# Sampling by matrix product in batches of three: twelve transposes, then three gathers, on six banks, with the exponent's table loaded at the start

## The reference

```
pos_y = base_y + inner_y + off_y            # clipped to 0 .. 17, the same for x
value = (hh*hw*v1 + hh*lw*v2 + lh*hw*v3 + lh*lw*v4) * mask
out   = einsum('nhwc,cf->nhwf', value, w)   # 9 taps x 64 channels -> 64
...
attn  = softmax(q @ k.T / sqrt(32));  o = attn @ v
...
c = h * c + sigmoid(i) * tanh(g);     h = sigmoid(o) * tanh(c)     # 256 steps
```

## Time and profile before

| | us |
|---|---|
| median of three runs | 424.03 (423.84 to 425.36) |
| the profiled execution | 425.57 |
| its span, first to last instruction | 423.8 |
| TensorE busy in the span | 399.5 (94%) |
| ScalarE busy | 262.9 (62%) |
| VectorE busy | 240.2 (57%) |
| GpSimd busy | 59.3 (14%) |
| mean granted TensorE clock | 0.994 of full |

### The profile page before, as it was taken

How to read it: one execution, slowest core, us unless ns; L and a number is a source line. 1 busy time by engine, 2 the same in 40 slices (tenths; PEclk the granted TensorE clock), 3 DMA queues, 4 the chain that set the end, 5 groups by cost and what they waited for, 6 DMA issues and landing times.

```text
span 423.8 us, 14792 instructions
## 1 busy us (share of the span) xinstructions
PE 399.5 (94%) x5669; PEld 215.5 (51%) x5669; DVE 240.2 (57%) x1161; ACT 262.9 (62%) x1127; POOL 59.3 (14%) x131
## 2 busy tenths in 40 slices
PE   8999998888999899999999999999899999999996
PEld 2555553545455455545555554555455545554332
DVE  2477745154565566656565656665566656565443
ACT  1676643563786587568748865876587568744443
POOL 6000004001111111012111102111111012110000
PEclk9999998999999999999999999999999999999999
DMA  7000000000000000000000000000000000000000
GB/s 243 0 2 2 2 2 0 0 2 2 3 3 2 4 6 2 4 2 5 5 2 5 4 2 4 5 3 3 2 6 3 2 2 7 3 3 5 2 2 5
DMA packets 2244, 3.78 MB, mean 9 GB/s; under 512 B 1277, under 2 KB 1726, under 8 KB 2174
## 3 DMA queue, kind: packets, MB, share of 16 engines
q1 hardware_dynamic: 1872, 2.32, 1.8%
q10 hardware_dynamic: 302, 0.52, 0.4%
HBM read 2.57 MB, written 0.26 MB: 7 GB/s over the span
## 4 chain that ended last, share of the span: by engine, by line
PE 69%; DVE 12%; ACT 12%; issue 5%; DMA 1%; POOL 1%; DVEq 0%
PE bank L349 20%; PE bank L620 15%; PE bank L478 7%; DVE bank L1036 5%; PE bank L416 5%; PE bank L404 5%; PE bank L489 4%; DVE H L1046 4%; ACT bank L760 4%; PE bank L506 3%; ACT bank L753 3%; PE bank L377 2%; ACT E L734 2%; ACT QB L726 2%; PE bank L518 1%
## 5 line engine op out<-in xcount | busy, mean ns | idle before, releaser
L349 PE MATMUL bank<-FB 128*128 128x512 bf16 (+3 forms) x677 | 184.4, 369 | 1.2 <-DVE FB L786 1.2
L620 PEld LDWEIGHTS bank<-H,VW 128*32 128x32 f32 x3072 | 53.0, 109 | 92.9 <-DVE H L1046 88.1
L620 PE MATMUL bank<-H,VW 128*32 128x4 f32 x3072 | 75.6, 179 | 12.6 <-DVE H L1046 5.6
L1036 DVE TENSOR_TENSOR_SCAN bank<-bank,SU 64x12 f32<-64x12 f32 x256 | 48.7, 190 | 64.9 <-ACT bank L753 62.2
L753 ACT ACTIVATE bank<-bank 64x8 f32<-64x8 f32 x256 | 37.9, 148 | 73.1 <-PE bank L620 72.1
L1046 DVE SCALAR_TENSOR_TENSOR H<-TO,bank 64x4 f32<-64x4 f32 x256 | 40.9, 160 | 49.2 <-ACT bank L760 47.4
L349 PEld LDWEIGHTS bank<-FB 128*128 128x128 bf16 x677 | 50.9, 99 | 31.4 <-issue 5.7
L760 ACT ACTIVATE bank<-bank 64x4 f32<-64x4 f32 x256 | 38.8, 152 | 17.6 <-DVE bank L1036 2.9
L757 ACT ACTIVATE TO<-bank 64x4 f32<-64x4 f32 x256 | 44.1, 172 | 6.3
L1030 DVE SCALAR_TENSOR_TENSOR SU<-H,bank 64x4 f32<-64x4 f32 x256 | 41.4, 162 | 9.0
L333 POOL TENSOR_SCALAR E<-E,rinv 128x256 f32<-128x256 f32 x56 | 27.0, 481 | 139.5 <-DVE rinv L909 139.5
(11 more groups left out here) (117 smaller groups left out, 341.1 us busy)
## 6 DMA issues: line engine op xcount, KB each, us to landing
AW<-in_attn_w SPq DMA_DIRECT2D x1, 768.5 KB, 8.1
DW<-in_dcn_w SPq DMA_DIRECT2D x1, 576.0 KB, 6.7
X<-in_x_fm SPq DMA_DIRECT2D x1, 256.0 KB, 3.3
X<-in_x_fm ACTq DMA_DIRECT2D x1, 256.0 KB, 5.2
out_dram<-OUT SPq DMA_DIRECT2D x8, 32.0 KB, 1.4
CW<-in_conv_w SPq DMA_DIRECT2D x1, 243.5 KB, 4.2
VEC<-in_vecs SPq DMA_DIRECT2D x1, 160.0 KB, 8.0
K<-in_consts ACTq DMA_DIRECT2D x1, 154.0 KB, 3.6
```

Of the source, the lines that this page charges most:

```text
L349: nc.tensor.matmul(idle[:, 0:n], FB[:, 0:P], FB[:, 0:n], start=True, stop=True)
L620: mm = nc.tensor.matmul(gate_out(m, gate, r, slice(B * s, B * (s + 1))), VW[:, gate, r], H[:, (STEPS * m + s - 1) % RING, :], start=False, ...
L1036: nc.vector.tensor_tensor_scan(CS.rearrange("p b q -> p (b q)"), GT.rearrange("p b q -> p (b q)"), SU[:].rearrange("p b q -> p (b q)"), 0. ...
```

## The change

Groups go through TensorE in threes. The loop issues the turns of three groups (twelve transposes), then the three gathers of the batch before. The first batch's turns are followed directly by the second's, and the last two batches' gathers stand together at the end. A, AT and the banks of the transposes become rings of six, and all waits that guard a slot are moved from 3 or 4 groups back to 6. The bank ring is now banks 1, 2, 0, 3, 6, 7; since Z went through banks 0, 3, 6 and 7, the wait for its 16 copies moves from gather(0) to turn(2) up to turn(5).

The second edit is a table load for Exp at the top of ScalarE's program, behind its three DMA issues; the load of the first tile at L763 is left out (`m > 0`).

```
+BATCH = 3
+SLOTS = 2 * BATCH
...
-        A = sb("A", [P, 4, HALVES, N])
-        AT = sb("AT", [P, 4, 2, HALVES, P])
+        A = sb("A", [P, SLOTS, HALVES, N])
+        AT = sb("AT", [P, SLOTS, 2, HALVES, P])
...
-        b_at = banks[1:4]
+        b_at = banks[1:3] + banks[0:1] + banks[3:4] + banks[6:8]
...
-                if g >= 3:
-                    pe.wait_ge(at_sb, g - 2)
+                if 2 <= g < SLOTS:
+                    pe.wait_ge(z_sb, 4 * B)
+                elif g >= SLOTS:
+                    pe.wait_ge(at_sb, g - SLOTS + 1)
...
-                        mm = nc.tensor.transpose(b_at[g % 3][:, P * q:P * (q + 1)],
-                                                 A[:, g % 4, h, P * pt:P * (pt + 1)], ident)
+                        mm = nc.tensor.transpose(b_at[g % SLOTS][:, P * q:P * (q + 1)],
+                                                 A[:, g % SLOTS, h, P * pt:P * (pt + 1)], ident)
...
-                if g == 0:
-                    pe.wait_ge(z_sb, 4 * B)
...
-            for g in range(len(GROUPS) + 1):
+            for g in range(0, len(GROUPS) + BATCH, BATCH):
                 if g < len(GROUPS):
-                    turn(g)
-                if g >= 1:
-                    gather(g - 1)
+                    for i in range(g, g + BATCH):
+                        turn(i)
+                if g >= BATCH:
+                    for i in range(g - BATCH, g):
+                        gather(i)
...
             act.dma_start(LW[:], lstm_w).then_inc(ld_lw, 16)
+            nc.scalar.preload_act_table(ACT.Exp)
...
-                if g >= 4:
-                    act.wait_ge(cv_mm, g - 3)
+                if g >= SLOTS:
+                    act.wait_ge(cv_mm, g - SLOTS + 1)
...
-                    if o == EXP_TABLE:
+                    if m > 0 and o == EXP_TABLE:
                         nc.scalar.preload_act_table(ACT.Exp)
...
-                if g >= 4:
-                    dve.wait_ge(at_mm, g - 3)
+                if g >= SLOTS:
+                    dve.wait_ge(at_mm, g - SLOTS + 1)
```

More of the change, by code:

```diff
@@ L416, in gather @@
                     mm = nc.tensor.matmul(b_cv[b % 2][C * pt:C * (pt + 1), 0:N], Z[:, pt, b, k, :],
-                                          AT[:, g % 4, pt, :, :], start=(k == 0), stop=(k == TAPS - 1))
+                                          AT[:, g % SLOTS, pt, :, :], start=(k == 0), stop=(k == TAPS - 1))
                 mm.then_inc(cv_mm, 1)
-            for g in range(len(GROUPS) + 1):
+            for g in range(0, len(GROUPS) + BATCH, BATCH):
                 if g < len(GROUPS):
-                    turn(g)
-                if g >= 1:
-                    gather(g - 1)
+                    for i in range(g, g + BATCH):
[3 more added lines that the diff above has]
+                        gather(i)
             pe.wait_ge(t0f_done, 2 * B)
@@ L697, in _ @@
                 act.wait_ge(at_mm, g + 1)
-                if g >= 4:
-                    act.wait_ge(cv_mm, g - 3)
-                nc.scalar.copy(AT[:, g % 4, :, :, :].rearrange("p a h q -> p (a h q)"), b_at[g % 3][:]
+                if g >= SLOTS:
+                    act.wait_ge(cv_mm, g - SLOTS + 1)
+                nc.scalar.copy(AT[:, g % SLOTS, :, :, :].rearrange("p a h q -> p (a h q)"), b_at[g % SLOTS][:]
                                ).then_inc(at_sb, 1)
@@ L861, in _ @@
                     distances(b + 2)
-                if g >= 4:
-                    dve.wait_ge(at_mm, g - 3)
+                if g >= SLOTS:
+                    dve.wait_ge(at_mm, g - SLOTS + 1)
                 sh = [P, HALVES, SIDE, SIDE]
-                nc.vector.tensor_tensor(A[:, g % 4, :, :].rearrange("p h (y x) -> p h y x", y=SIDE),
+                nc.vector.tensor_tensor(A[:, g % SLOTS, :, :].rearrange("p h (y x) -> p h y x", y=SIDE),
                                         HAT[:, 0, b, k, :, :, None].to_broadcast(sh),
```

## The result

The changed kernel takes 414.93 us (414.82 to 415.21, four runs) against 424.49 us of the kernel before on the same chip: a ratio of 0.9775, interval 0.9754 to 0.9796, 9.6 us off. Forecast were 414.9 us and 9.1 us off.

What follows compares the result with a forecast made beforehand. TensorE alone was taken to bound the sampling, at 1.17 us a group, with a table load before the queries. Gains of 7.8 + 1.3 = 9.1 us off 424.0 gave 414.9 us; 8-in-10 range 413.3 to 418.6.

Steps and rivals of the forecast that it cites:

- The sampling, 7.8 us: From first transpose to last gather: fewer changes of kind save 7.2 us, vanished stalls some 0.5; gain taken as 7.8 us.
- 0.44 and 0.43 us a group: TensorE in the sampling: four transposes cost 0.44 us, a gather 0.43 us, as before the change.
- the seams between gathers: Sampling, gather after gather with a wait between: 24 seams, taken as zero, at most 0.15 us each, 3.6 us in all.
- the end stalls: First and last gather of the sampling waited for their copies; both stalls go, some 0.5 us.
- The Z wait: Before turn(2): last Z copy ends by 23.22, turn(2) can begin at 23.49, so the moved wait is hidden by 0.27 us.
- The table load, 1.28 us: Between key copies and queries on ScalarE: without the load the first scores begin earlier and all behind shifts, 1.28 us.
- The clock in the layer norm, nothing: Half-level clock from 67.46 to 70.87: counted as nothing if it moves or goes, since Y's last transposes wait for VectorE.
- The gap belongs to going from transposes to products: Sampling on TensorE: going from transposes to gathers and back costs 0.30 us a round.
- Seams: Rival, sampling: a gather's waiting weight load is not fetched ahead, 3.6 us come back, 418.5 us; 12%.
- a load hidden elsewhere: Rival, at the queries: something else takes up the table load's time, 1.28 us are lost, 416.2 us; 7%.
- waits as the cause: Rival, sampling: the gap belongs to waits, so batching brings nothing and only the load counts, 422.7 us; 3%.
- The falling clock: Rival, sampling: twelve transposes in a row drop TensorE to half clock; slower, 446 us if throughout; 3%.

Runs made afterwards that it cites:

- the wide gather: The kernel before, still alternating, its gather made four passes one behind the other with weights 128 columns wide: 429.26 us, 1.0098.
- 24 transposes in a row: The changed kernel with batches of 3, 3, 3, 3, 6, 6, 6, 6 and twelve slots: 416.39 us; with one sum three groups later, 414.06 us.
- the twelve profiles of the table: Profiles of the kernel before, the changed kernel (twice), each edit alone, and variants in ring, batch size or gather width; times 414.1 to 439.3 us.

## Why the prediction was right, and where its reason was not

- *The sampling, 7.8 us.* Right: 7.83. Its parts too: 0.44 and 0.43 us a group are what twelve and three take (1.46 and 1.45 us with their half of the round), the seams between gathers cost nothing, the end stalls went, and no engine but TensorE came into the chain. The Z wait moved to turn(2) hid: 22 transposes follow without a break from 21.99.
- *The table load, 1.28 us.* Right: 1.31.
- *The clock in the layer norm, nothing.* Right. Before, it was at half level from 67.46 to 70.87; in the changed kernel it stayed up; the stretch is 9.20 and 9.19 us.
- *The gap belongs to going from transposes to products.* This is what the prediction said a round is ("the price of going from transposes to gathers and back"), and it is wrong. The border that costs is between a product that takes a part of the columns and an operation that takes all. The number was right all the same because here the two borders are the same; that is the kernel's doing and not the reason's. The trace had the hint:

```profile
22.13 0.65 PE L377 MATMUL bank<-DW,XC 128*128 128x288 f32 x2
22.37 1.04 PEld L404 LDWEIGHTS bank<-K,A 128*128 128x128 f32 x8
```

  From the last Z product (128 columns) to turn(0) the weights of the transposes were loaded at 22.37, at once, and turn(0) followed at 22.61 without a gap, although this border is between a product and a transpose. The other hint is L518 above: a gap between two products. A reader of the prediction would have expected the wide gather to take 439 us; it took 429.
- *The rivals.* Seams (12%), a load hidden elsewhere (7%) and waits as the cause (3%) are refuted by the changed kernel's trace. The falling clock (3%) too: even 24 transposes in a row kept the full level in the sampling. So the Trainium skill's remark that transposes don't count as a busy TensorE in the same way (page TensorE: Matmul & The Clock Gate, Part 4) did not come to bear at this length.
- *The base, and luck.* The two stretches give 9.14 us; the rest up to 9.56 is not in them. The kernel before takes from 423.84 to 425.85 us over all its unprofiled executions, and a gain from medians moves with that: against 424.03, the base of the prediction, it would be 9.1. That 414.9 was met to 0.1 us is luck as well. In two later measurements the changed kernel took 415.75 and 416.11 us, where the kernel before took 424.62 and 425.31. And for a profiled execution the prediction had 416.5 us, with the last gather near 57.3; it took 414.90, with the last gather at 56.2. It carried over the long start and recurrence of the profiled execution of the kernel before, and here these were 1.00 and 0.5 us shorter.

## What to carry to other kernels

Where small products on a part of the array's columns alternate with work on the whole array, look for a price at each border: in this kernel a round of the two cost TensorE 0.30 us, under whatever name the profile gave the idle time. Put several of a kind in a row; the buffers this needs are a means and gained nothing alone. When a batch grows, look first at what another engine has queued in program order behind its wait for the batch before. And when a sum is right, still part its causes: two that always come together in one kernel give the same number there and different ones in the next.

## What the runs showed of the hardware

- Not every narrow operation pays. Transposes with 64 columns of weights (L442) alternate with fill products over all 128 columns in the changed kernel at 0.11 us each, without a gap:

```profile
63.50 0.11 PE bank L351
63.61 0.11 PE bank L442
63.72 0.11 PE bank L351
```

  So the width of the weights alone does not make the gap. Why transposes are exempt from what a product of 64 columns pays was not tried.
- This kernel's start is not steady: the granted clock reached 2.4 GHz between 3.9 and 10.3 us from the start, and in the two profiles of the changed kernel (spans 413.1 and 414.4 us, clock up at 5.6 and 10.3) 1.28 of the 1.3 us between them lie ahead of the first transpose. Over the twelve profiles of the table, the four whose clock rose after 9 us have a start of 22.61 us or more and the eight others of 22.38 or less, but within the eight the order does not hold (3.9 and 21.99, but 5.6 and 21.61). The clock is the likeliest cause and not a shown one.
